# Expert outputs scattered tile by tile, and a regrouped step between two quantised attention passes

## The chip, the cores and the metric

The kernel runs on one core of a Trainium2 chip. The metric is device time in microseconds (us) from the start to the end of one execution. Three runs of the kernel before gave 2891.12, 2894.81 and 2895.28 us; their median is 2894.81 us. The profile comes from one further execution, which took 2868.81 us, with a span of 2867.1 us between its first and last record.

## The reference, cut to what matters

The model is a small tower: token embedding with a trace memory, linear attention, a soft mixture of experts, an attention block whose operands are fake-quantised to 8 bits, and last a transformer block with attention and a mixture of 8 experts of which each token uses two. There are B = 8 sequences of S = 512 tokens with D = 192 features. Two parts matter here.

```python
# quantised attention: per-tensor scale from the largest absolute value
def fake_quant(x, bits=8):
    scale = jnp.maximum(jnp.max(jnp.abs(x)) / 127.0, 1e-08)
    return jnp.clip(jnp.round(x / scale), -128, 127) * scale
attn = jnp.einsum('bhnd,bhmd->bhnm', fake_quant(q), fake_quant(k)) * scale
attn = fake_quant(jax.nn.softmax(attn, axis=-1))
out = jnp.einsum('bhnm,bhmd->bhnd', attn, fake_quant(v))

# routed experts: each token's two best experts, weighted by a softmax of their logits
top_logits, top_idx = jax.lax.top_k(xn @ gate_w, 2)
gates = scatter(softmax(top_logits))
y = gelu(xn @ w1[e] + b1[e]) @ w2[e] + b2[e]
out = x + sum over the two experts of gates * y
```

The softmax of the quantised attention has one scale for the whole tensor, so its maximum over all rows must be known before a single probability can be rounded. That is why this attention makes two passes over the scores.

## The kernel before, in words

The program is a list of stages, each made of blocks. In a block every engine has its own instruction list; the lists are written out by hand and run in order, engines meet only through semaphores, and all engines meet at the end of a block. Loops written with `Fori` are loops of the chip, others are unrolled. DMAs that `sp` issues go through SyncE's queue, those that `pool` issues through GpSimd's. `Link` (line 89) makes an instruction signal and the next one wait for it.

**Linear attention** (line 442) also fills the DRAM tensor `routed_in` with zeros (line 483), long before it is used, since the expert tiles are padded.

**Quantised attention** (line 1321). Pass 1 (lines 1641 to 1673) computes scores with queries on the partitions, takes each row's maximum (`MXq`) and, on ScalarE, the sum of exponentials (`RS`). Then a block of its own prepares pass 2 (lines 1684 to 1739): VectorE takes 1/RS and its maximum over all rows, GpSimd reduces it over partitions, and from it and ScalarE's logarithm follows one number for each query row, by which pass 2 shifts its scores so that the exponential gives the probability already in units of the quantisation step. The shift is split into three bf16 parts (`BP`, lines 1698 and 1703), turned by 32 TensorE transposes (1728), copied out of PSUM to `BT` (1707) and laid by DMA into three spare rows under each head's query features in `QI` (1738). Twelve heads sit in three groups `g` of four slots `q` of 32 partitions. Pass 2 (lines 1752 to 1844) computes the scores turned, with K spread by DMA into `QM` (1762) and V copied to `VS` (1764); the same five DMAs are made for each of the 8 sequences, two buffers alternating.

**Routed experts** (line 2368). After a layer norm (`XA` holds the rows) and the gate logits, one block works out for each of the 4096 tokens and its 2 experts a place `POS` in a list sorted by expert, in 39 tiles of 256 rows. GpSimd then sends the rows with 64 indirect DMAs of 128 rows (line 2532) to `routed_in`. The tile block (2609 to 2726) runs 39 tiles: SyncE loads a tile's rows (2621, 2622) and its expert's weights (2505, a ring of `NW` = 4), TensorE turns them (2652), multiplies by W1 (2662, 2666), ScalarE applies gelu (2701), TensorE multiplies by W2 (2677), VectorE adds the bias (2718), and GpSimd stores the tile to `routed_out` in sorted order (2637) and waits for the store before it frees the buffer `YM`. A last block gathers: 64 indirect DMAs (2739) fetch each token's two output rows by `POS`, VectorE adds both, weighted, to the residual (2751, 2755), and SyncE stores the result (2767).

## Time and profile before

| | |
|---|---|
| median of 3 runs | 2894.81 us |
| the profiled execution / its span | 2868.81 / 2867.1 us |
| busy: TensorE, VectorE, ScalarE, GpSimd | 69%, 53%, 39%, 11% of the span |
| between pass 1 and pass 2 of the quantised attention | 1334.6 to 1385.8 us |
| sending the rows to the experts | 2343 to 2426 us |
| the 39 tiles | 2426 to 2775 us |
| the last block | 2775 to 2867 us |

Shares of busy time are averages over stages with different limits. A change in one stage is judged by that stage's own rows: what ran, and what was waited for. The chain that ended last, as the profile follows it, covers only the last block here, so the other stages are read from the timeline.

### The profile page before, as it was taken

To read this page: it belongs to the slowest core of one execution; us is meant where nothing else is said; L and a number is where in the kernel's file an instruction comes from. 1 tells how busy PE (TensorE), PEld (TensorE's weight loads), DVE (VectorE), ACT (ScalarE), POOL (GpSimd) and SP (SyncE) were. 2 spreads that over 40 slices of the span, in tenths; PEclk is the share of its full clock that TensorE was granted. 3 is DMA by queue.
4 is the path that set the end of the run, shared out by engine and by line. 5 is a ranking of instruction groups with operands and counts; after the bars stand their busy time and mean duration, and the time that the engine had idled before them with its cause. 6 is when DMAs were issued, how large, how long until landed. Compare 5 with 4: busy or idle time off the path is not lost. (4 is left out here: it accounts for less than half of the span.)

```text
span 2867.1 us, 32319 instructions
## 1 busy us (share of the span) xinstructions
PE 1967.8 (69%) x9516; PEld 1035.9 (36%) x9538; DVE 1521.2 (53%) x2573; ACT 1124.2 (39%) x1862; POOL 312.9 (11%) x338
## 2 busy tenths in 40 slices
PE   4787788678873436664577648885799740999960
PEld 3645645353341100000111223321233340888850
DVE  4366378640026668886477738896477640111113
ACT  1102222231113579996588622220688410322210
POOL 4000000001110000000000042220000026000026
PEclk9899989777865655555799767775899755999985
DMA  3041100138930000000100048772898022455533
GB/s 71 11 137 39 42 17 22 54 146 311 411 151 11 0 15 11 11 11 2 36 26 29 1 77 114 105 105 30 117 111 109 3 95 79 174 200 209 202 105 107
DMA packets 140738, 251.39 MB, mean 88 GB/s; under 512 B 28762, under 2 KB 108251, under 8 KB 135628
## 3 DMA queue, kind: packets, MB, share of 16 engines
q1 hardware_dynamic: 128340, 225.99, 30.8%
q0 software_dynamic: 12304, 24.20, 2.9%
q8 instruction: 52, 0.85, 0.1%
q14 instruction: 42, 0.34, 0.0%
HBM read 194.69 MB, written 38.04 MB: 81 GB/s over the span
## 5 line engine op out<-in xcount | busy, mean ns | idle before, releaser
L1641 PE MATMUL ps<-arena 128*128 x376 | 194.3, 620 | 158.6 <-ACT ps L1673 96.0
L1673 ACT ACTIVATE ps<-ps,arena 128x512 f32<-128x512 f32 x384 | 291.8, 993 | 9.7 <-DVE arena L1652 9.7
L1658 DVE TENSOR_REDUCE arena<-ps 128x1024 f32 x192 | 234.4, 1224 | 47.9 <-PE ps L1641 46.5
L2032 DVE TENSOR_REDUCE arena<-ps 128x1024 f32 (+1 forms) x192 | 226.8, 1221 | 47.2 <-PE ps L2148 42.8
L1819 ACT ACTIVATE arena<-ps,arena 128x1024 f32<-128x1024 f32 x192 | 197.8, 1111 | 36.6 <-DVE arena L1841 27.3
L2313 ACT ACTIVATE arena<-ps 128x1024 f32<-128x1024 f32 x192 | 185.2, 1022 | 38.2 <-PE ps L2250 36.4
L2148 PE MATMUL ps<-arena 96*128 96x512 bf16 x384 | 159.7, 509 | 36.6 <-DVE arena L2032 23.6
L531 PE MATMUL ps<-arena 96*128 96x456 f32 (+1 forms) x512 | 176.5, 498 | 9.3 <-DMA arena<-arena 5.7
L2701 ACT ACTIVATE arena<-ps,arena 128x256 f32<-128x256 f32 x234 | 89.5, 481 | 235.9 <-PE ps L2666 235.9
L1841 DVE TENSOR_SCALAR arena<-arena 128x1024 bf16<-128x1024 f32 x192 | 130.8, 691 | 95.6 <-ACT arena L1819 79.0
L2718 DVE TENSOR_TENSOR arena<-ps,arena 128x384 f32<-128x384 f32 x39 | 21.7, 557 | 289.4 <-PE ps L2677 289.4
L1673 ACT ACTIVATION_READ_ACCUMULATOR ps<-ps,arena 128x1 f32 x384 | 171.6, 447 | 0.0
L2677 PE MATMUL ps<-arena 128*128 128x192 f32 x936 | 162.5, 331 | 0.7 <-DVE arena L2718 0.7
L2677 PEld LDWEIGHTS ps<-arena 128*128 128x128 f32 x936 | 151.0, 190 | 13.6 <-issue 13.6
L1781 PE MATMUL ps<-arena 128*128 (+1 forms) x370 | 117.3, 398 | 39.1 <-DMA arena<-arena 36.4
L1641 PEld LDWEIGHTS ps<-arena 128*128 128x128 bf16 x384 | 26.0, 112 | 326.3 <-ACT ps L1673 228.3
L2250 PE MATMUL ps<-arena 99*128 99x512 bf16 x384 | 103.2, 389 | 38.4 <-DMA arena<-arena 34.0
L531 PEld LDWEIGHTS ps<-arena 96*128 96x128 f32 x512 | 100.5, 205 | 76.6 <-issue 58.8
L2662 PE MATMUL ps<-arena 128*128 128x256 f32 x468 | 109.4, 384 | 0.9 <-ACT arena L2701 0.9
L1799 PE MATMUL ps<-arena 128*32 128x512 bf16 x384 | 77.5, 400 | 46.8 <-DVE arena L1841 38.6
L2288 PE MATMUL ps<-arena 128*32 128x512 f32 x768 | 103.5, 611 | 3.3 <-ACT arena L2313 3.3
L1204 DVE COPY arena<-ps 128x768 f32<-128x768 f32 x16 | 15.3, 957 | 159.9 <-PE ps L1246 159.9
(370 smaller groups left out, 3265.4 us busy)
## 6 DMA issues: line engine op xcount, KB each, us to landing
arena<-in_sm_w_dram SPq DMA_DIRECT2D x128, 576.0 KB
arena<-in_re_w_dram SPq DMA_DIRECT2D x39, 1252.0 KB, 5.7
arena<-ra_parts SPq DMA_DIRECT2D x192, 192.0 KB, 9.8
ra_parts<-arena SPq DMA_DIRECT2D x48, 192.0 KB, 2.5
routed_in<-arena SPq DMA_DIRECT2D x1, 7488.0 KB, 26.4
arena<-routed_in SPq DMA_DIRECT2D x39, 192.0 KB, 5.5
routed_out<-arena POOLq DMA_DIRECT2D x39, 192.0 KB, 2.3
arena<-la_xt SPq DMA_DIRECT2D x16, 384.0 KB, 3.3
```

The source lines that it names most:

```text
L531: ins = pe.matmul(ps[:, 2 * (t % 2) + bank, to:to + w], XTs[j][:, c, t * P:(t + 1) * P], Wx[:, kind, c, at:at + w], start=(c == 0), stop=( ...
L1641: ins = pe.matmul(ps[:, 2 * (n % 4) + t % 2, :], QM[j][:, h, t * P:(t + 1) * P], KI[:, b, h // HG, :], start=True, stop=True)
L1658: v.tensor_reduce(MXq[:, b, h, 2 * u:2 * u + 2], ps[:, 2 * (n % 4):2 * (n % 4) + 2, :], AX.X, ALU.max).then_inc(s_lk, 1)
L1673: ins = act.activation(bank, bank, ACT.Exp, bias=nb[n % 4][:, t % 2:t % 2 + 1], scale=c_exp, accum_out=RS[:, b, h, t:t + 1])
L1781: ins = pe.matmul(ps[:, 2 * (n % 3) + q, :], QM[j][:, h, c * P:(c + 1) * P], QI[:, bass.ds(b, 1), g, :].rearrange("p o s -> p (o s)"), sta ...
L1819: act.activation(PF[n % 2], ps[:, 2 * (n % 3):2 * (n % 3) + 2, :].rearrange("p a s -> p (a s)"), ACT.Exp, scale=c_exp).then_inc(pe_.sem, 1)
L1841: v.tensor_scalar(PB[n % 2], PF[n % 2], MAGIC, MAGIC, ALU.add, ALU.subtract).then_inc(rd.sem, 1)
L2032: v.tensor_reduce(MX[:, bass.ds(b, 1), 2 * (n % 2):2 * (n % 2) + 2, n // 2].rearrange("p o t -> p (o t)"), ps[:, 2 * (n % 2):2 * (n % 2) + ...
L2148: ins = pe.matmul(ps[:, t, :], ST_[j][0][0:KR, h, t * P:(t + 1) * P], ST_[j][1][0:KR, h, :], start=True, stop=True)
L2313: act.activation(PF[e // 2 % 2][:, 2 * (e % 2):2 * (e % 2) + 2, :], ps[:, 2 * (e % 3):2 * (e % 3) + 2, :], ACT.Exp, scale=HD ** -0.5).then ...
L2662: pe.matmul(unit(k), wr[:, k * P:(k + 1) * P], XT[j][:, 0, :], start=True, stop=False)
L2677: ins = pe.matmul(ps[:, 7, h * D:(h + 1) * D], HT[j][:, k, h * P:(h + 1) * P], wr[:, at:at + D], start=(k == 0), stop=(k == KH - 1))
```

## The change

**Shift rows.** The minimum of `RS` is taken and then one reciprocal of a 128 x 1 column, instead of 384 reciprocals per partition and a maximum. `RS` and `MXq` are laid out so that heads are innermost; the three casts and two subtractions each become one instruction over 128 x 384. The transposes now leave the three parts of one head in neighbouring rows of `BT`; the copy out of PSUM is halved between VectorE and ScalarE; and the 36 DMAs of one row become 12 DMAs of three rows. The K and V copies for the first two sequences of pass 2 are issued at the start of this block, and pass 2's loop starts at its third sequence.

**Routing.** Rows of `routed_in` grow from 192 to `RW` = 196 words; the first word is the number of the row of `routed_out` to which this row returns. GpSimd writes that word into `XA` with an iota for each of the two experts, so the 64 indirect DMAs are now ordered by expert choice `k`, and the second iota waits until the first 32 DMAs have landed. Padding rows carry numbers of spare rows, written in the earlier fill. In the tile block VectorE copies the two numbers per partition to `back` (four buffers), and GpSimd issues two indirect DMAs per tile (128 rows each) that scatter the tile's rows to token order, in place of one plain store. The row load waits for the copy of the turned rows (`xc`) instead of the transposes (`xt`), since `back` is read from the same buffer. In the last block 16 plain loads replace the 64 gathers, its loops are unrolled, and ScalarE's queue stores the result.

```diff
-            l(v.reciprocal(W_, RS))
-            v.tensor_reduce(pmax, W_, AX.XYZ, ALU.max).then_inc(s_b, 1)
+            l(v.tensor_reduce(pmax, RS, AX.XYZ, ALU.min))
+            v.reciprocal(pmax, pmax).then_inc(s_b, 1)
...
             for k in range(3):
-                for b in range(B):
-                    ins = v.tensor_copy(BP[:, b, :, k, :], turned(W_, b))
-                    if b == B - 1:
-                        l(ins)
+                l(v.tensor_copy(BP[:, :, :, k], W_))
                 if k < 2:
-                    for b in range(B):
-                        ins = v.tensor_tensor(turned(W_, b), turned(W_, b), BP[:, b, :, k, :], ALU.subtract)
-                    l(ins)
+                    l(v.tensor_tensor(W_, W_, BP[:, :, :, k], ALU.subtract))
...
-            v.tensor_copy(BT.rearrange("p (u b) s -> p u (b s)", u=4),
-                          ps[0:3 * NH, 0:4, :].bitcast(BF16)).then_inc(s_bc, 1)
+            v.tensor_copy(BT[:, 0:4, :].rearrange("p (u b) s -> p u (b s)", u=2),
+                          ps[0:3 * NH, 0:2, :].bitcast(BF16)).then_inc(s_bc, 1)
...
+            act.wait_ge(s_bt, 2)
+            act.activation(BT[:, 4:8, :].rearrange("p (u b) s -> p u (b s)", u=2),
+                           ps[0:3 * NH, 2:4, :].bitcast(BF16), ACT.Copy).then_inc(s_bc, 1)
...
-            for k in range(3):
-                for h in range(NH):
-                    row = 32 * (h % HG) + HD + k
-                    sp.dma_start(QI[row:row + 1, :, h // HG, :], BT[k * NH + h:k * NH + h + 1, :, :]
-                                 ).then_inc(s_q, 16)
+            for j in range(2):
+                spread(sp, j, j)
+            sp.wait_ge(s_bc, 2)
+            for q in range(HG):
+                for g in range(NG):
+                    row, at = 32 * q + HD, 3 * (q * NG + g)
+                    sp.dma_start(QI[row:row + 3, :, g, :], BT[at:at + 3, :, :]).then_inc(s_q, 16)
...
             for k in range(2):
-                pool.wait_ge(s_sc[k], 16 * NR)
+                if k:
+                    pool.wait_ge(s_sc[0], 16 * NR)
+                pool.iota(to_row, [[S, B], [1, T]], base=k * NT * P, channel_multiplier=T).then_inc(s_tr, 1)
+                pool.wait_ge(s_tr, k + 1)
+                if not k:
+                    pool.wait_ge(s_pl, 1)
+                for n in range(NR):
+                    pool.indirect_dma_start(xd, bass.IndirectOffsetOnAxis(ap=POS[:, n, k:k + 1], axis=0),
+                                            XA[:, n // T, n % T, :], None).then_inc(s_sc[k], 16)
...
             def load_rows(n):
-                xt.wait(sp, n, -1)
+                xc.wait(sp, n, -1)
...
-                pool.dma_start(yd_t[n], YM[j]).then_inc(m.ym[j], 16)
-                pool.wait_ge(m.ym[j], 16 * (n // 2 + 1))
+                for h in range(2):
+                    pool.indirect_dma_start(yd, bass.IndirectOffsetOnAxis(ap=back[n % 4][:, h:h + 1], axis=0),
+                                            YM[j][:, h, :], None).then_inc(m.ym[j], 16)
+                pool.wait_ge(m.ym[j], 32 * (n // 2 + 1))
...
             def rows(n):
                 xt.wait(v, n, 1)
+                if n >= 4:
+                    yf.wait(v, n, -3)
+                v.tensor_copy(back[n % 4], XM[n % 2].bitcast(I32)[:, :, 0])
                 hp.wait(v, n, -3)
...
-                v.wait_ge(s_y, b + 1)
+                v.wait_ge(s_g[b], 32)
...
+            for b in range(B):
+                for k in range(2):
+                    at = (k * B + b) * S
+                    sp.dma_start(Y[:, b, k, :, :], rows_of(yd[at:at + S])).then_inc(s_g[b], 16)
```

On SyncE's queue, in the block between the two passes, stood before (a row is a line, what it issues, its shape, and how often in a run; the last rows are the head of pass 2's loop):

```order
L1732 UNCONDITIONAL_BRANCH
L1738 DMA arena<-arena 1x8x512 x36
L1684 UNCONDITIONAL_BRANCH
L1754 UNCONDITIONAL_BRANCH
L1757 UNCONDITIONAL_BRANCH
L1757 ISA
L1762 ISA
```

The same place now, where 1758 is the line of the shift rows, 1699 of the K copies and 1701 of the V copies:

```order
L1750 UNCONDITIONAL_BRANCH
L1699 DMA arena<-arena 32x3x512 x4
L1701 DMA arena<-arena 128x1536
L1699 DMA arena<-arena 32x3x512 x4
L1701 DMA arena<-arena 128x1536
L1758 DMA arena<-arena 3x8x512 x12
L1703 UNCONDITIONAL_BRANCH
L1770 UNCONDITIONAL_BRANCH
L1772 UNCONDITIONAL_BRANCH
L1772 ISA
```

Ten copies moved ahead of the shift rows, and 36 DMAs of 1 x 8 x 512 became 12 of 3 x 8 x 512.

GpSimd's list from the sending of the rows (2532) over the tile stores (2637) to the last block's gathers (2739), before:

```order
L2524 AFFINE_SELECT arena<-arena 128x128
L2532 DMA routed_in<-arena 9984x192 x64
L2507 UNCONDITIONAL_BRANCH
L2631 UNCONDITIONAL_BRANCH
L2637 DMA routed_out<-arena 128x384 x39
L2616 UNCONDITIONAL_BRANCH
L2734 UNCONDITIONAL_BRANCH
L2739 DMA arena<-routed_out,arena 128x192 x64
```

The same stretch now, with the iotas on line 2543, the sending on 2548 and the scatter of the tiles on 2653:

```order
L2537 AFFINE_SELECT arena<-arena 128x128
L2543 IOTA arena 128x32
L2548 DMA routed_in<-arena 9984x196 x32
L2543 IOTA arena 128x32
L2548 DMA routed_in<-arena 9984x196 x32
L2520 UNCONDITIONAL_BRANCH
L2646 UNCONDITIONAL_BRANCH
L2653 DMA routed_out<-arena 8448x192 x78
L2631 UNCONDITIONAL_BRANCH
```

The 64 gathers of the last block are gone from this list; 39 more DMAs stand in the tile block, and an iota stands in the middle of the sending.

## Rows read from the trace of the kernel before

**Rows 1.** Windows: length, busy PE, PEld, DVE, ACT, POOL, clock, DMA share, GB/s
```profile
2339.00:2356.00 17.00, 0.00 (x0) 0.00 (x0) 2.81 (x8) 0.00 (x0) 10.00 (x11) 0.50 0.91 353
2500.00:2700.00 200.00, 200.00 (x1207) 176.16 (x1205) 27.54 (x48) 52.79 (x138) 12.94 (x24) 1.00 0.58 201
2774.70:2867.10 92.40, 0.00 (x0) 0.00 (x0) 29.51 (x72) 0.00 (x0) 63.76 (x64) 0.50 0.33 102
```

**Rows 2.** Timeline between the passes: start, duration, engine, line, idle before and its releaser
```profile
1334.94 2.55 DVE L1688 RECIPROCAL arena<-arena 128x384 f32<-128x384 f32 x1 [3.71 <-PEq L1616]
...
1338.57 0.15 DVE L1691 TENSOR_SCALAR arena<-arena 128x1 f32<-128x1 f32 x1 [0.49 <-POOL arena L1713]
...
1339.48 0.62 DVE L1694 SCALAR_TENSOR_TENSOR arena<-arena 128x384 f32<-128x384 f32 x1 [0.56 <-ACT arena L1718]
1340.14 0.97 DVE L1698 CAST arena<-arena 128x48 bf16<-128x48 f32 x8
...
1345.85 3.57 PE L1728 MATMUL ps<-arena 128*36 128x128 bf16 x32 [16.26 <-DVEq L1705]
1349.46 2.28 DVE L1707 COPY arena<-ps 36x4096 bf16<-36x4096 bf16 x1 [3.76 <-PE ps L1728]
1351.77 26.02 SPq L1738 DMA_DIRECT2D arena<-arena  x36
1378.90 1.28 ACT L1819 ACT_TABLE_LOAD   x1 [39.53 <-DVEq L134]
1379.40 3.08 SPq L1762 DMA_DIRECT2D arena<-arena  x4
...
1385.80 2.34 PE L1781 MATMUL ps<-arena 128*128 128x512 bf16 x5 [36.38 <-DMA arena<-arena]
...
1386.47 3.14 ACT L1819 ACTIVATE arena<-ps,arena 128x1024 f32<-128x1024 f32 x3 [6.28 <-PE ps L1781]
```

**Rows 3.** Line 1604, the one earlier DMA on three partitions: issue durations
```profile
L1604 SPq DMA_DIRECT2D arena<-arena x4: 786/1582/3449, 1023.2 to 1027.3; - x4
```

**Rows 4.** The same DMAs, by window while they move (columns as in rows 1)
```profile
1025.50:1035.50 10.00, 0.00 (x0) 0.00 (x0) 0.00 (x0) 1.28 (x1) 0.00 (x0) 0.50 0.20 34
```

**Rows 5.** Timeline of the last block and the store before it
```profile
2772.42 0.54 POOL L2637 DMA_DIRECT2D routed_out<-arena  x1 [4.34 <-DVE arena L2718]
2775.22 0.96 DVE L2751 TENSOR_TENSOR arena<-arena  x1 [3.10 <-PEq L2616]
...
2790.09 0.95 POOL L2739 DMA_INDIRECT arena<-routed_out,arena  x1 [0.30 <-issue]
...
2791.35 1.22 POOL L2739 DMA_INDIRECT arena<-routed_out,arena  x1 [0.30 <-issue]
...
2862.07 1.40 DVE L2755 SCALAR_TENSOR_TENSOR arena<-arena  x4 [0.18 <-DVE arena L2755]
```

**Rows 6.** DMA issues by kind: queue, count, KB each, median us from issue to landing
```profile
arena<-la_xt SPq DMA_DIRECT2D x16, 384.0 KB, 3.3
routed_out<-arena POOLq DMA_DIRECT2D x39, 192.0 KB, 2.3
arena<-routed_out,arena POOLq DMA_INDIRECT x64, 2.6
```

**Rows 7.** Line 2532: issue durations in ns, first and last start, landing
```profile
L2532 POOL DMA_INDIRECT routed_in<-arena x64: 956/960/1199, 2343.0 to 2422.9; - x64
...
DMA to landing us min/median/max: 2.3/2.3/7.4
```

**Rows 8.** Timeline, one tile of the loop, VectorE, GpSimd and SyncE
```profile
2560.19 0.56 DVE L2718 TENSOR_TENSOR arena<-ps,arena 128x384 f32<-128x384 f32 x1 [7.47 <-PE ps L2677]
...
2561.04 0.54 POOL L2637 DMA_DIRECT2D routed_out<-arena  x1 [8.08 <-DVE arena L2718]
2561.49 0.36 SPq L2505 DMA_DIRECT2D arena<-in_re_w_dram  x1
...
2569.66 0.54 POOL L2637 DMA_DIRECT2D routed_out<-arena  x1 [8.09 <-DVE arena L2718]
```

More of the change, by code:

```diff
@@ L1673, in _, with spread @@
                         ins = act.activation(bank, bank, ACT.Exp, bias=nb[n % 4][:, t % 2:t % 2 + 1],
-                                             scale=c_exp, accum_out=RS[:, b, h, t:t + 1])
+                                             scale=c_exp, accum_out=RS[:, b, t, at_head(h):at_head(h) + 1])
                     ins.then_inc(ex.sem, 1)
     g4 = Cut(m.arena, mark, END)
-    BP = g4(P, [B, T, 3, NH], BF16)
+    BP = TMP[:, S:S + 3 * B * T * NH // 2].bitcast(BF16).rearrange("p (n h k) -> p n h k", h=NH, k=3)
     BT = g4(3 * NH, [B, S], BF16)
-    W_ = TMP[:, 0:B * NH * T].rearrange("p (b h t) -> p b h t", b=B, h=NH)
+    W_ = TMP[:, 0:B * NH * T].rearrange("p (n h) -> p n h", h=NH)
+    rows = lambda a: a.rearrange("p b t h -> p (b t) h")
     s_a, s_b, s_c, s_ln, s_bp, s_bt, s_bc, s_q = (sem(f"qa_shift_{n}") for n in (
         "chain", "max", "max_of_all", "log", "parts", "turned", "copied", "rows"))
+    km = [sem(f"qa_k_spread{j}") for j in range(2)]
+    def spread(sp, b, j):
+        for q in range(HG):
+            sp.dma_start(QM[j][32 * q:32 * q + 32].rearrange("p (g j) s -> p g j s", j=HG)[:, :, q, :],
+                         KI[32 * q:32 * q + 32, b, :, :]).then_inc(km[j], 16)
+        sp.dma_start(VS[j], VI[:, b, :, :, :]).then_inc(km[j], 16)
     with nc.Block(no_gpsimd_drain=True) as block:
@@ L1755, in _ @@
         def _(sp):
-            sp.wait_ge(s_q, 16 * 3 * NH)
-            with sp.Fori(0, B // 2) as i:
+            with sp.Fori(1, B // 2) as i:
                 for j in range(2):
-                    b = 2 * i + j
                     prev(sp, av, i, j)
-                    for q in range(HG):
-                        sp.dma_start(QM[j][32 * q:32 * q + 32].rearrange("p (g j) s -> p g j s", j=HG)[:, :, q, :],
-                                     KI[32 * q:32 * q + 32, b, :, :]).then_inc(km[j], 16)
-                    sp.dma_start(VS[j], VI[:, b, :, :, :]).then_inc(km[j], 16)
+                    spread(sp, 2 * i + j, j)
         @block.tensor
@@ L2420, in norm @@
                 ins.then_inc(xa.sem, 1)
[L2422 removed]
+                rows = XA[:, bass.ds(b, 1), :, HEAD:RW].rearrange("p o t d -> p (o t) d")
                 xa.wait(v, b, 1)
@@ L2606, in routed_experts @@
     two = lambda shape: [w(P, shape) for _ in range(2)]
-    XM, XT, HT, YM = two([2, 2 * P]), two([2, TR]), two([KH, TR]), two([2, D])
+    XM, XT, HT, YM = two([2, HEAD + 2 * P]), two([2, TR]), two([KH, TR]), two([2, D])
+    back = [w(P, [2], I32) for _ in range(4)]
     xm = [sem(f"re_rows_loaded{j}") for j in range(2)]
@@ L2764, in _ @@
         def _(sp):
-            with sp.Fori(0, B) as b:
-                sp.wait_ge(s_f, b + 1)
-                sp.dma_start(io.out[bass.ds(b, 1)].rearrange("o (p t) d -> (o p) (t d)", t=T),
-                             m.H[:, b, :, :].rearrange("p t d -> p (t d)")).then_inc(s_o, 16)
-            sp.wait_ge(s_o, 16 * B)
+            for b in range(B):
+                for k in range(2):
+                    at = (k * B + b) * S
+                    sp.dma_start(Y[:, b, k, :, :], rows_of(yd[at:at + S])).then_inc(s_g[b], 16)
+        @block.scalar
+        def _(act):
+            for b in range(B):
+                act.wait_ge(s_f, b + 1)
+                act.dma_start(rows_of(io.out[b]), m.H[:, b, :, :]).then_inc(s_o, 16)
+            act.wait_ge(s_o, 16 * B)
 def kernel_program(nc, io):
```

91 lines of the change are left out of this document (40 added, 51 removed).

## The prediction

> **What bounds the kernel now.** I read the windows first [rows 1]. While the tiles run, TensorE is busy in all 200 of 200 us at full granted clock (2.4 GHz), GpSimd in 12.9: what the change adds to GpSimd there has room, and nothing there can be won. In the last block TensorE is idle, VectorE is busy 29.5 of 92.4 us and GpSimd 63.8: the gathers set its pace. Then the timeline between the two passes [rows 2]: from the reciprocal at 1334.94 to the first exponential of pass 2 at 1386.47 there is one chain and nothing beside it. Its longest link is SyncE's 36 DMAs, 26.02 us at 0.72 each. Every microsecond cut from these two chains comes off the end, since all engines meet at the end of a block.
>
> **The step between the passes, VectorE's part.** The reciprocal falls from 384 elements to one: from 2.55 us to about the 0.15 of a 128 x 1 operation, -2.4. The minimum costs what the maximum did. The split took from 1340.14 to 1345.85, 5.7 us. Now it is three casts and two subtractions of 128 x 384, each at most the 0.62 of the SCALAR_TENSOR_TENSOR of that size, together 3.1, -2.6. The transposes (3.57 us) stay. Of the copy (2.28 us for 4096 columns) VectorE's half hides beside the second 16 transposes; ScalarE's half of 2048 columns comes behind them. One ScalarE instruction of 1024 columns takes 1.05 us (3.14 for three), so at most 2.1, and no less than half of VectorE's 2.28, 1.14. I take 2.1, by the ScalarE row: -0.2. The shift rows can then start at 1351.77 - 5.2 = 1346.6 [rows 2].
>
> The ten K and V copies now ahead of them on SyncE's queue are issued from 1335 on: four take 3.08 us [rows 2], all ten about 7.5, so they are through at 1342.5, under VectorE's chain.
>
> **The shift rows.** By the issue alone, 12 times 0.72 make 8.7 us. Each DMA now carries three rows of 8 KB. The only earlier DMA on three partitions is line 1604: four of 72 KB, whose issues took 0.79, up to 3.45 us [rows 3], so SyncE was held up by the transfer. While they moved, the DMA share was 0.20, about three engines of 16, and the rate 34 GB/s [rows 4]. The 288 KB of the shift rows at 34 GB/s take 8.7 us as well, as long as the issues. The upper end is line 1604's own pace: 0.79, 3.45 and two around the median of 1.58 make 7.4 for four, 1.85 each, 22.2 for twelve, though those carry three times the bytes. Below 8.7 I see no way, because SyncE must issue twelve. I take 10.2, near the lower end, since by bytes the two limits agree and only their overlap is imperfect.
>
> The Trainium skill (DMA: Bandwidth & Descriptors, section "Why a DMA increments its semaphore by 16 and not by 1") says that the engines of a DMA are the largest number up to 16 that divides both slowest dimensions. By that rule a 3 x 8 x 512 transfer uses three engines where a 1 x 8 x 512 used eight; it speaks against the regrouping, and the share of 0.20 agrees with it. It would make the transfer, not the issue, the limit, which is the first rival.
>
> The issues end at 1356.8. Now the next DMA that waits for the rows starts 1.6 us after the last issue ended (1377.79 to 1379.40), so the rows have landed at 1358.4; the first matmul about 0.4 later (my allowance for waking TensorE and its weight load), and the exponential 0.67 behind it as now (1385.80, 1386.47) make 1359.5. ScalarE's table load began 1.1 us after the last issue and takes 1.28 [rows 2]: done at 1359.2, just covered. The K and V copies that stood here (1379.40 to 1385) are already in place. Pass 2 starts at 1359.5 and not 1386.47: **-27.0**. The ends are -29.5 (ScalarE's copy at 1.14, transfer at 8.7) and -15.0 (22.2 for the DMAs). The changed layouts of `MXq` and `RS` move writes of two elements or one; pass 1 and pass 2 keep their pace.
>
> **The last block.** Now it begins 2.8 us after the last store is issued (2772.42, 2775.22). A second DMA 1.26 us behind the first (0.95 + 0.30 [rows 5]) and a landing of 2.6 instead of 2.3 us [rows 6] put the begin at 2776.8. The second of the two loads for the first sequence is issued 0.6 later and lands 3.3 us on, as the 384 KB load from DRAM does [rows 6]: 2780.7, first weighted sum at 2780.8. A sequence then costs VectorE 0.96 + 1.40 + 0.18 + 1.40 = 3.94 us [rows 5]. The first sum pair takes 3.0, seven more sequences 27.6: 2811.4. From VectorE's last instruction (2863.5) to the end now is 3.6 us. End at 2815.0 against 2867.1: **-52.1**.
>
> What could hold this back is the transfer: 6.3 MB in and 3.1 MB out. At 353 GB/s, as the four weight loads moved [rows 1], that is 26.7 us, less than VectorE's 3.0 + 27.6, but not by much. At the 201 GB/s of the tile loop, which there is demand and not a limit [rows 1], it would be 47 us, and the block 13 longer than forecast: -39. The other end is -54, if the first loads land in 1.3 us less.
>
> **Sending the rows.** The 64 issues keep 1.27 us (2343.0 to 2422.9, 63 steps [rows 7]); 784 instead of 768 bytes a row don't matter to an issue-bound stretch. New is the stop between `k` = 0 and 1: instead of one step of 1.27 the last landing of 2.3 [rows 7], the iota with its signals, 0.4, and a first issue of 1.2 against 0.96. **+1.7**, between +1 and +3. The first iota stands ahead of the wait for `POS`.
>
> **The tiles.** Per tile VectorE gets one more copy of 128 x 2, about 0.15 us, and idles 7.5 [rows 8]; it counts only ahead of the first tile, where both turns wait for it: **+0.4**, ends 0 and 1. The row load waits about 0.7 us longer for its tile, but it is issued well over a tile ahead, behind a wait for `yc` that ends later. GpSimd: one store at 0.54 us becomes two scatters, 0.95 + 0.30 + 0.95. It starts at 2561.04, and the next tile is due at 2569.66 [rows 8]. The second scatter is issued at 2562.3; with 2.3 to 2.6 us of landing [rows 6, 7] GpSimd is free at 2565, 4.6 us early. But the weights start at 2561.49. With weights under way, a scatter of line 2532 landed in up to 7.4 us [rows 7]; there four experts' weights were queued, here one's. Then it would be free at 2569.8, 0.2 to 0.5 us late. I take nothing. New on VectorE is that the copy to `back` waits for the store of the tile before the last; queued behind it are the copy of the turned rows, for which TensorE waits only a tile later, and the next bias addition.
>
> The Trainium skill (SBUF — State Buffer, section "SBUF: two separate sides") says that GpSimd can't write descriptors while VectorE runs a two-port copy. This trace shows up to 0.27 us of it (1.22 instead of 0.95 while VectorE works [rows 5]); in the tile loop it would lie in GpSimd's 4.6 spare us, and the sum would be the same.
>
> **The sum.** -27.0 - 52.1 + 1.7 + 0.4 = -77.0. The profiled execution of 2868.8 us becomes 2791.8. The runs' median lies 26.0 above it; I keep that distance: 2894.8 - 77.0 = 2817.8, so 2818.
>
> **The rivals.**
> 1. Three-partition transfers set the pace: line 1604's held-up issues speak for it, the equal 8.7 us by bytes against. At the middle of the two ends, 16 us instead of 10.2: 2824; at the full 22.2, 2830.
> 2. The last block is bound by its transfers: all 16 loads are queued at once and the stores share the engines; against it stand 353 GB/s and long contiguous runs. At 201 GB/s, 2831.
> 3. The scatter paces the tiles mildly: a landing of 7.4 us makes the cycle 0.5 us longer than TensorE's 8.62, times 39 is +20: 2838. Against it: one expert's weights are a quarter of what stood before that 7.4.
> 4. Slower than before: the same place in earnest. GpSimd waits for both scatters before it frees `YM`, VectorE waits for that, TensorE for VectorE. The 77 us are lost when the cycle reaches 8.62 + 77/39 = 10.6 us, that is a landing of about 9. If scattered rows of 768 bytes among the weights landed in 10 us, it would be 11.7 and +120: 2938. No row shows such a landing.
> 5. It doesn't do what it says: the loads can't start early or the shift rows cost as before. Then only one of the two large terms comes, 2845 to 2870.
>
> **Chances.** Forecast 0.64, rivals 0.11, 0.10, 0.08, 0.04, 0.03. The best ends together give 29.5 + 54 - 1 = 82.5, 2812; the distance of 26 us to the runs is uncertain by their spread of 4, so I start the range at 2808. Upward it takes in rivals 1 to 3: 2838. What a measurement can tell from no change is 0.2%, 6 us. Only rival 4, below its full price too, can come out there or beyond: faster 0.94, same 0.02, slower 0.04.
>
> **What would show it.** In the profile after: first exponential of pass 2 about 25 us after the minimum; the twelve issues in 9 to 11 us (right) or 16 and more (rival 1); eight sequences at 3.9 us each in the last block, VectorE not waiting for loads; a single gap of about 3 us in the sending; tiles still 8.62 us apart with TensorE busy throughout. Tiles further apart than 8.8, or a last block over 45 us, would make the prediction wrong.

## The result, and the profile after

The kernel after takes 2802.77 us (median of 4 runs, 2798.69 to 2814.05) against 2894.06 us before, a ratio of 0.9692 with a 95% interval of 0.9663 to 0.9721: 91 us less, where the forecast was 77. It lies 5 us under the low end of the forecast range. The direction and the main mechanism were forecast, the time was not.

The windows of the kernel after, in the columns of [rows 1]: the twelve shift-row DMAs, the tile loop and the last block.

```profile
1356.00:1366.00 10.00, 0.00 (x0) 0.00 (x0) 0.00 (x0) 0.00 (x0) 0.00 (x0) 0.54 0.13 27
...
2500.00:2700.00 200.00, 200.00 (x1208) 176.28 (x1207) 28.36 (x69) 54.07 (x142) 44.09 (x46) 1.00 0.60 204
2763.10:2800.60 37.50, 0.00 (x0) 0.00 (x0) 29.54 (x72) 0.00 (x0) 0.00 (x0) 0.50 0.67 252
```

The tile loop is what it was, TensorE busy throughout, with GpSimd at 44 instead of 13 us of 200. The last block is 37.5 us long, VectorE busy in 29.5 of them (before in 29.5 of 92.4), and the transfers run at 252 GB/s.

The step between the passes, timeline of the kernel after (it answers to [rows 2]):

```profile
1344.82 2.66 SPq L1699 DMA_DIRECT2D arena<-arena  x4
...
1344.86 0.55 DVE L1707 TENSOR_REDUCE arena<-arena 128x1 f32<-128x384 f32 x1 [3.71 <-PEq L1625]
1345.44 0.16 DVE L1708 RECIPROCAL arena<-arena 128x1 f32<-128x1 f32 x1
...
1350.53 3.26 PE L1745 MATMUL ps<-arena 128*36 128x128 bf16 x32 [11.02 <-DVEq L1719]
...
1353.83 1.87 ACT L1734 ACTIVATE arena<-ps 36x2048 bf16<-36x2048 bf16 x1 [6.92 <-PE ps L1745]
1355.72 9.77 SPq L1758 DMA_DIRECT2D arena<-arena  x12
1366.42 1.28 ACT L1830 ACT_TABLE_LOAD   x1 [10.73 <-DVEq L136]
1368.53 0.13 PEld L1792 LDWEIGHTS ps<-arena 128*128 128x128 bf16 x2 [14.92 <-DMA arena<-arena]
...
1369.61 2.12 ACT L1830 ACTIVATE arena<-ps,arena 128x1024 f32<-128x1024 f32 x2 [1.90 <-PE ps L1792]
```

From the minimum to the first exponential: 24.75 us (forecast 24.6; before 51.5). The twelve issues take 9.77.

The last block, timeline of the kernel after (it answers to [rows 5]):

```profile
2759.21 0.96 POOL L2653 DMA_INDIRECT routed_out<-arena  x1 [2.66 <-DVE arena L2738]
2760.47 0.96 POOL L2653 DMA_INDIRECT routed_out<-arena  x1 [0.30 <-issue]
2763.11 8.96 SPq L2776 DMA_DIRECT2D arena<-routed_out  x16
2763.15 0.96 DVE L2759 TENSOR_TENSOR arena<-arena 128x768 f32<-128x768 f32 x1 [4.22 <-PEq L2631]
2767.16 2.85 DVE L2763 SCALAR_TENSOR_TENSOR arena<-arena 128x192 f32<-128x192 f32 x8 [3.05 <-DMA arena<-routed_out]
...
2771.50 2.85 DVE L2763 SCALAR_TENSOR_TENSOR arena<-arena 128x192 f32<-128x192 f32 x8 [0.62 <-DMA arena<-routed_out]
...
2775.25 2.85 DVE L2763 SCALAR_TENSOR_TENSOR arena<-arena 128x192 f32<-128x192 f32 x8
```

The first weighted sum comes 4.0 us after the begin, as forecast; a sequence then takes 3.75 us (2771.50 to 2775.25; forecast 3.94, because the 0.18 us between two groups of four is gone). Behind the first load, which the forecast waited for too, only the second sequence waits, 0.62 us.

Sending and one tile, GpSimd, VectorE and SyncE of the kernel after (they answer to [rows 7] and [rows 8]):

```profile
2368.41 0.96 POOL L2548 DMA_INDIRECT routed_in<-arena  x1 [0.30 <-issue]
2370.80 0.18 POOL L2543 IOTA arena<- 128x32 int32 x1 [1.44 <-DMA routed_in<-arena]
2371.26 0.98 POOL L2548 DMA_INDIRECT routed_in<-arena  x1 [0.28 <-POOL arena L2543]
...
2564.24 0.56 DVE L2738 TENSOR_TENSOR arena<-ps,arena 128x384 f32<-128x384 f32 x1 [7.39 <-PE ps L2694]
2564.71 0.16 DVE L2730 COPY arena<-arena 128x2 int32<-128x2 int32 x1
...
2565.07 0.96 POOL L2653 DMA_INDIRECT routed_out<-arena  x1 [6.40 <-DVE arena L2738]
...
2566.33 0.96 POOL L2653 DMA_INDIRECT routed_out<-arena  x1 [0.30 <-issue]
...
2572.86 0.56 DVE L2738 TENSOR_TENSOR arena<-ps,arena 128x384 f32<-128x384 f32 x1 [7.40 <-PE ps L2694]
```

One gap of 2.85 us from issue to issue in the sending; the tiles are 8.62 us apart, as before.

Where the time lies, as differences between the first instructions of the stages. The middle column is the kernel before, unchanged, in another execution (run e1 below).

| us | before, trace shown | before, run e1 | after |
|---|---|---|---|
| embedding stage | 136.6 | 145.5 | 146.2 |
| to the end of pass 1 | 1198.4 | 1198.3 | 1198.6 |
| minimum to first exponential | 51.5 | 51.5 | 24.8 |
| pass 2 | 227.0 | 226.9 | 228.6 |
| to the routing's first iota | 709.9 | 710.3 | 710.9 |
| iota to last sending DMA | 99.6 | 99.6 | 101.4 |
| to the first bias addition | 25.2 | 25.1 | 24.4 |
| 39 tiles | 323.5 | 323.5 | 323.5 |
| last bias addition to the end | 95.5 | 110.7 | 42.2 |
| span | 2867.1 | 2891.4 | 2800.6 |

The first and third columns differ by the forecast's terms, -26.8 and -53.3 among them, and by +9.6 us in a stage that the change doesn't touch. The first two columns are the same kernel, and differ in two rows: 8.9 and 15.2 us.

### The profile page after: what moved, and what is told of

Read it like the earlier page. It is cut to its first block and busy times, and to the rows that moved or that the text cites. A ratio compares the mean times of both kernels' runs of the same rounds, so it can differ in the third digit from the quotient of the medians.

```text
span 2800.6 us, 32083 instructions
## 1 busy us (share of the span) xinstructions
PE 1964.5 (70%) x9516; PEld 1031.1 (37%) x9538; DVE 1518.9 (54%) x2578; ACT 1125.9 (40%) x1863; POOL 302.7 (11%) x316
## 5 line engine op out<-in xcount | busy, mean ns | idle before, releaser
L1650 PEld LDWEIGHTS ps<-arena 128*128 128x128 bf16 x384 | 25.6, 110 | 326.6 <-ACT ps L1682 228.6
L2653 POOL DMA_INDIRECT routed_out<-arena x78 | 74.8, 958 | 275.2 <-DVE arena L2738 256.2
## 6 DMA issues: line engine op xcount, KB each, us to landing
routed_in<-arena SPq DMA_DIRECT2D x1, 7644.0 KB, 24.6
```

The source lines that it names most:

```text
L1650: ins = pe.matmul(ps[:, 2 * (n % 4) + t % 2, :], QM[j][:, h, t * P:(t + 1) * P], KI[:, b, h // HG, :], start=True, stop=True)
```

## The experiments

### The parts, and the kernel before once more (e1 to e4, on one chip)

e1 is the kernel before, unchanged.

> The kernel before, unchanged, profiled once more. The question is why its timed runs (2891 to 2895 us) lie 25 us above its one profiled execution (2868.8), while the timed runs of the changed kernel lie around its profiled one. Theory A (the profiled execution was an unusually short one; upstream stages vary from one execution to the next): the new profiled execution comes out near 2893, and its trace shows the extra 20 to 25 us in stages that the change does not touch, the embedding stage first (136.6 us in the trace shown). Theory B (the profiler itself shortens or lengthens this program): the new profiled execution is again near 2869 while the timed ones stay near 2893.

Measured: 2893.16 us (10 runs), 2894.36 for the same kernel beside it, span 2891.4. The execution first shown was a short one; so far theory A, though the runs further below put it down to the chip and not to the execution. But its missing time lies in two places, the embedding stage and the last block, and the second belongs to what the change removes.

e2 has the new step between the passes alone; of the change's diff, for one:

```diff
-                    sp.dma_start(QI[row:row + 1, :, h // HG, :], BT[k * NH + h:k * NH + h + 1, :, :]
-                                 ).then_inc(s_q, 16)
...
+                    sp.dma_start(QI[row:row + 3, :, g, :], BT[at:at + 3, :, :]).then_inc(s_q, 16)
```

> Only the step between the two quantised passes is changed. By the traces the step gives 26.8 us and pass 2 takes 1.9 of them back, so theory A expects 24 to 28 us less than before, about 2867 where before is at 2893. A rival by which the timed gain of 91 us hides a larger effect of this step than its trace shows expects 35 us or more.

Measured: 2866.24 us, ratio 0.9895 (0.9878 to 0.9913), 28 us less, the upper edge of theory A's range. First exponential 24.91 us after the minimum for 51.5, pass 2 1.7 us longer.

e3 has the routing alone (rows that carry their address, the scatter in each tile, plain loads at the end), and the step between the passes as before:

```diff
+                    pool.indirect_dma_start(yd, bass.IndirectOffsetOnAxis(ap=back[n % 4][:, h:h + 1], axis=0),
+                                            YM[j][:, h, :], None).then_inc(m.ym[j], 16)
...
+                    sp.dma_start(Y[:, b, k, :, :], rows_of(yd[at:at + S])).then_inc(s_g[b], 16)
```

> Only the routing is changed (rows carry their return row, tiles are scattered, the last block loads plain rows). By the traces: last block and its begin -53.3, sending +1.6, tile loop about 0: 51 to 53 us less, about 2841 where before is at 2893. A rival by which the unexplained 14 us of the timed gain belong to the routing (for example to instruction fetch in the looped last block) expects 65 us less.

Measured: 2825.55 us, ratio 0.9761 (0.9745 to 0.9777), 69 us less. My expectation failed; the rival named in it, that the unexplained time belongs to the routing, is what happened.

e4 is the kernel after.

> The changed kernel, unchanged, profiled once more. Theory A (the embedding stage varies between executions) expects that its embedding stage does not take 146.2 us again to a tenth, and the total moves with it by some us; a rival (the changed program always has the longer embedding stage, through where its instructions lie) expects 146 us again, and 137 in the kernel before.

Measured: 2800.42 us, ratio 0.9679 (0.9663 to 0.9695), 94 us less; the parts make 28 + 69 = 97. Its embedding stage takes 143.7 us, not 146.2, as theory A expected, but the kernel before has 145.5 there in e1 and not 137. So the stage is long in both kernels, and its length varies.

What differs in the last block of before between its two executions stands in a view of one line's instructions (min/median/max in ns, first and last start). Line 2755 in the execution first shown, and behind it in e1:

```profile
L2755 DVEq FUSED_REGOPS  x96: 65/93/105, 2787.6 to 2862.4; - x96
L2755 DVE SCALAR_TENSOR_TENSOR arena<-arena x64: 408/412/420, 2787.9 to 2863.1; - x64
```

```profile
L2755 DVEq FUSED_REGOPS  x96: 1/93/1396, 2796.6 to 2886.7; - x96
L2755 DVE SCALAR_TENSOR_TENSOR arena<-arena x64: 408/415/477, 2796.9 to 2887.3; - x64
...
  issue: 48.7, 21
```

Line 2749, the loop's own, in e1:

```profile
L2749 DVEq ALU_OP  x8: 11/40/700, 2799.0 to 2886.9; - x8
L2749 DVEq COMPARE_BRANCH  x8: 40/56/700, 2799.0 to 2886.9; - x8
```

The timeline of e1 from the last gather on, GpSimd and VectorE:

```profile
2866.08 0.94 POOL L2739 DMA_INDIRECT arena<-routed_out,arena  x1 [0.30 <-issue]
...
2870.44 0.42 DVE L2755 SCALAR_TENSOR_TENSOR arena<-arena  x1 [2.39 <-issue]
2872.62 1.12 DVE L2755 SCALAR_TENSOR_TENSOR arena<-arena  x3 [1.76 <-issue]
...
2886.35 1.41 DVE L2755 SCALAR_TENSOR_TENSOR arena<-arena  x4 [0.18 <-DVE arena L2755]
```

The arithmetic is as fast as ever, and the gathers are too: the last one is issued 82 us into the block in both. But from 2810.9 to 2873.2, 46 of the 62 register and branch instructions of VectorE and SyncE take 0.70 us each (one 1.40) for 0.04 to 0.10. From 2819.9 on their starts lie on one grid of 0.70 us, for both engines alike: SyncE's at 2826.3, 2827.7 and 2829.1, VectorE's at 2826.3, 2828.4, 2829.8 and 2831.2. The same grid shows in e2 and e13. Without the slow ones, VectorE ends 4.9 us behind the last gather (2858.55 to 2863.47); with it, 20.7 us. From 2876 on, the gathers landed, a pair of groups is back at 3.0 us.

### Loop and gathers, one without the other (e5, e6, e13, e16)

e5 is the kernel before with the loops of VectorE and SyncE in the last block written out:

```diff
-            with v.Fori(0, B) as b:
-                link = Link(v, s_a, b * 2)
+            link = Link(v, s_a)
+            for b in range(B):
...
-                       scalar=GT[:, bass.ds(T * b + t, 1), k], in1=m.H[:, b, t, :],
+                       scalar=GT[:, T * b + t, k:k + 1], in1=m.H[:, b, t, :],
...
-            with sp.Fori(0, B) as b:
+            for b in range(B):
```

> The kernel before with one edit: in the last block VectorE's loop over the 16 sequences and SyncE's loop of stores are written out, so that neither engine has register or branch instructions there; the 128 gathers of GpSimd stay. In every new execution of the kernel before, these register instructions took 0.70 us each beside the gathers (46 of them, 33 us) and the block 107 us; in the execution that the forecast started from none did and the block took 92 us. Theory A (these instructions, slowed beside the gathers, are what the forecast missed): 15 us less, a median of 2878 us (2874 to 2882), the block again at 92 us, the embedding stage as before at 144 to 147 us. Rival B (everything on VectorE is slowed there and the register instructions are only where it is seen): other instructions take over the time, the block stays at 105 to 107 us and the median at 2889 to 2896 us.

Measured: 2879.35 us (2875.93 to 2882.62), 15.0 less than the 2894.33 beside it; block 92.1 us, embedding stage 146.6. Theory A in all three numbers. (The kernel has 64 gathers and 8 sequences here; the 128 and 16 above, and the 16 in e6, are slips.)

e6 is the kernel after with the loop back, and no gathers:

```diff
+            with v.Fori(0, B) as b:
+                link = Link(v, s_a, b * 2)
-                v.wait_ge(s_g[b], 32)
+                v.wait_ge(s_y, b + 1)
...
+        @block.gpsimd
+            for b in range(B):
+                pool.wait_ge(s_g[b], 32)
+                pool.sem_inc(s_y, 1)
```

> The kernel after with one edit: in the last block VectorE's code is a loop over the 16 sequences again, with register instructions, while GpSimd issues no gather there (it only passes a semaphore on). Theory A (register instructions are slow only beside GpSimd's indirect DMAs): each takes under 0.1 us, the block takes 38 to 41 us for 37.4, and the median is 1 to 3 us above the kernel after (2801 to 2806 us). Rival B (a loop is slow in this place whatever GpSimd does, 0.70 us for each of some 46 register instructions): 10 to 15 us more, a median of 2811 to 2816 us.

Measured: 2804.91 us (2804.47 to 2806.91), block 40.4 us for 37.4, as theory A expected, and its register instructions are short:

```profile
L2763 DVEq FUSED_REGOPS  x96: 65/93/99, 2766.4 to 2798.2; - x96
```

So it takes both: loop with gathers 107.0 us, gathers without loop 92.1, loop without gathers 40.4, neither 37.4. The loop costs 15 us beside the gathers and 3 without them.

e13 (the kernel before, unchanged) and e16 (e5's kernel) ran on a third chip, after a chip had shown the lower level (below).

> The kernel before, unchanged, for its trace on this chip. Theory A (the two levels belong to the chip): its time is that of all runs of the kernel before beside it, near 2869 or near 2893 us; at the lower level no register instruction of the last block takes over 0.1 us, that block takes 92 us and the embedding stage 134 to 138 us; at the upper level 46 take 0.70 us, the block takes 107 us, the stage 144 to 147 us. Rival B (the levels belong to single executions): both kinds show among the runs of one chip.

> The kernel before with the last block's VectorE and SyncE loops written out, once more. Theory A (the 15 us that this saved were register instructions, slowed beside the gathers on chips of the upper level alone): on a chip where the kernel before takes 2869 us it takes 2865 to 2870 us, nothing or at most a few us less; where that takes 2893 us, 2876 to 2882 us. Rival B (the loop costs its 15 us everywhere): 2854 us on the first kind.

Measured: e13 2893.87 us, block 107.0, stage 147.7; e16 2875.57 us (2874.97 to 2881.38), 19 less than the 2894.34 beside it, block 89.7. Theory A's upper level in both; the times between this chip's runs don't mix the levels. e16 lies 0.4 us below the range given.

### The embedding stage (e7)

The kernel after with VectorE's loop there written out:

```diff
-                with v.Fori(B // 4 * half, B // 4 * (half + 1)) as i:
+                for i in range(B // 4 * half, B // 4 * (half + 1)):
```

> The kernel after with one edit: VectorE's loop over pairs of sequences in the embedding stage is written out. Nine or ten of its register instructions take 0.70 to 0.84 us each beside GpSimd's gathers of embedding rows in every execution but the one that the forecast started from (6.3 to 8.4 us in all; the stage takes 144 to 147 us for 136.6 us there). Theory A: the stage is back at 136.5 to 139 us, and the median 6 to 9 us lower than that of the kernel after, 2791 to 2795 us. Rival B (the gathers set the stage's pace and VectorE's slow instructions lie in its waits): less than 2 us, 2799 to 2802 us.

Measured: 2798.38 us (2794.92 to 2802.18), 2 us under e4's 2800.42 and not told from it (the ratios, each to the kernel before on its own chip, are 0.9674 and 0.9679). Theory A failed. Rival B's range is missed by 0.6 us, which the spread of the runs doesn't settle. The slow register instructions are gone, and yet the stage takes 142.9 us (143.7 in e4, and 147.2 in e15, which has the same edit). Something else holds it. ScalarE's instruction for the second sequence, in the first trace of before, then in the kernel after:

```profile
44.15 0.49 ACT L324 ACTIVATE arena<-ps 128x384 f32<-128x384 f32 x1 [4.72 <-PE ps L358]
```

```profile
51.12 0.49 ACT L326 ACTIVATE arena<-ps 128x384 f32<-128x384 f32 x1 [11.92 <-remote]
```

In e7, ScalarE and VectorE both stand still and start within 0.04 us of each other:

```profile
42.81 0.81 PE L360 MATMUL ps<-arena 128*128 x2
...
50.79 1.25 DVE L278 TENSOR_SCALAR arena<-arena 128x192 f32<-128x192 f32 x4 [12.57 <-remote]
50.83 0.49 ACT L326 ACTIVATE arena<-ps 128x384 f32<-128x384 f32 x1 [11.96 <-remote]
```

Both wait for TensorE, whose products end at 43.6, and both go on at 50.8, about 3 us after the last gather of the embedding (47.08 + 0.95). This pause of 7 us is in all 15 traces from chips whose kernel before took 2893 to 2898 us, with ScalarE's start at 50.8 to 51.3, and in none of the other five. The trace's own record of the semaphore says where it arises: the increment that VectorE waits for belongs to a product that ends at 42.98, and is recorded at 50.76. It is 7.0 to 9.0 us behind its product in those 15 traces, 0.01 to 0.02 in the other five. So by these records the signal is late, and not the engines that wait for it.

The same traces lack records. The 32 gathers of this stage raise their semaphores 512 times (16 each); 231 to 254 of these are recorded in the 15 traces, 507 to 512 in the other five. So one rival is open: that on these chips the recording itself holds the engines up. Every run here, timed ones too, has a span that comes from such records, and no run without them stands against it.

### Two levels, by chip (e14, e17, e18)

On the chip of e9 to e12, the kernel before took 2869.29 us in the median of 15 runs (2861.66 to 2874.75). On the five other chips of these experiments it took 2887.0 to 2902.2 in all of 69 runs. None of the four traces from that chip has a register instruction over 0.5 us, nor the pause (ScalarE's instruction starts at 42.4 to 43.7), and their embedding stage takes 133.9 to 137.7 us. The trace that the forecast started from is of this kind (2868.81 us); the runs shown beside it were of the other. To get the kernel after on such a chip, it went to further chips:

> The kernel after, unchanged. Theory A: on a chip where the kernel before takes 2869 us, it takes 2791 to 2795 us (the sum of the forecast, 77 us less, a ratio of 0.973); on a chip where that takes 2893 us, 2799 to 2803 us (94 us less, a ratio of 0.9675). Rival B (the change is worth the same on both kinds of chip): 2775 us on the first kind.

> The kernel after, unchanged, on one more chip. Theory A (the level belongs to the chip): where the kernel before beside it takes 2869 us, 2791 to 2795 us, a ratio of 0.973; where that takes 2893 us, 2799 to 2803 us and 0.968. Rival B (the change is worth 94 us everywhere): 2775 us and 0.967 on the first kind.

> The kernel after, unchanged, on one more chip. Theory A (the level belongs to the chip): where the kernel before beside it takes 2869 us, 2791 to 2795 us, a ratio of 0.973; where that takes 2893 us, 2799 to 2803 us and 0.968. Rival B (the change is worth 94 us everywhere): 2775 us and 0.967 on the first kind.

Measured: all of the upper level, 2801.64, 2799.31 and 2803.07 us; ratios 0.9680 (0.9655 to 0.9705), 0.9671 (0.9655 to 0.9687) and 0.9672 (0.9656 to 0.9688). The ratio is the same on every chip of that kind. The kernel after itself was not run at the lower level, so what theory A and rival B say of it stayed untested. The nearest is e9, 2798.33 us there; its duplicates cost 4.6 us behind the last tile and nothing in the tiles, so after would take 2793.7, 75.6 less than before. From e11 (below), 2794.04 us with a step 4.9 us longer, it would be 2789.1, 80 less. Both are worked out, not measured.

### The prices in the forecast (e8 to e12, e15)

e8: the kernel after, its 12 three-row DMAs cut into 36 of one row.

```diff
-                    sp.dma_start(QI[row:row + 3, :, g, :], BT[at:at + 3, :, :]).then_inc(s_q, 16)
+                        sp.dma_start(QI[row:row + 1, :, g, :], BT[at:at + 1, :, :]).then_inc(s_q, 16)
```

> The kernel after with the 12 DMAs of three partition rows each between the quantised passes cut into 36 of one row each; the bytes are the same. Theory A (SyncE's issues set the pace of these copies, 0.76 us each with a floor of 0.61 us): 24 more issues, the first exponential of pass 2 comes 15 to 18 us later than the 24.8 us after the minimum, the median 2815 to 2819 us. Rival B (what is paid is the bytes through the SBUF side of three partitions, and the issues only queue behind it): the exponential 0 to 3 us later, the median 2800 to 2804 us.

The issues in e8's timeline:

```profile
1354.29 26.01 SPq L1759 DMA_DIRECT2D arena<-arena  x36
```

Measured: 2814.80 us (2810.41 to 2815.93); first exponential 39.3 us after the minimum for 24.8. Theory A's mechanism, with both numbers just under its ranges (14.5 us for 15 to 18): 0.60 us for each further issue.

e9 and e10: each tile's scatters twice and three times.

```diff
-                for h in range(2):
-                    pool.indirect_dma_start(yd, bass.IndirectOffsetOnAxis(ap=back[n % 4][:, h:h + 1], axis=0),
+                for h, y in [(h, y) for y in [yd] + io.spare for h in range(2)]:
+                    pool.indirect_dma_start(y, bass.IndirectOffsetOnAxis(ap=back[n % 4][:, h:h + 1], axis=0),
```

> The kernel after with twice the scatters: in each tile GpSimd issues four indirect DMAs for two, the second pair with the same rows and the same indices into a spare tensor that nobody reads. Theory A (the scatters run in slack: a tile's 8.62 us are set elsewhere, and n scatters close their cycle in about 0.26 + 1.264 n + 2.3 to 2.6 us): four close in 7.3 to 7.7 us, the tiles stay 8.62 us apart and the median within 2 us of the kernel after (2799 to 2804 us). Rival B (the scatters' bytes or descriptors slow the other transfers or VectorE): the tiles come more than 0.1 us further apart, over 4 us in all, 2805 us or more.

> The kernel after with three times the scatters (six indirect DMAs for two in each tile, four of them into two spare tensors that nobody reads). Theory A: six close their cycle in 9.8 to 10.2 us, GpSimd sets the pace of the 39 tiles, the 8.62 us become 9.8 to 10.2 and the median 2846 to 2862 us. Rival B (the buffers of two tiles let the landing overlap with the next tile's issue, so that only 6 x 1.264 = 7.6 us of issue count): no change, 2799 to 2804 us.

Measured: e9 tiles still 8.62 us apart; 2798.33 us; e10 10.29 us apart, 2876.07 us. GpSimd, e9 then e10:

```profile
2505.52 0.96 POOL L2653 DMA_INDIRECT routed_out<-arena  x1 [3.83 <-DVE arena L2738]
...
2509.32 0.96 POOL L2653 DMA_INDIRECT spare<-arena  x1 [0.31 <-issue]
2514.22 0.96 POOL L2653 DMA_INDIRECT routed_out<-arena  x1 [3.93 <-DMA spare<-arena]
```

```profile
2504.11 0.96 POOL L2653 DMA_INDIRECT routed_out<-arena  x1 [3.15 <-DMA spare<-arena]
...
2510.43 0.96 POOL L2653 DMA_INDIRECT spare<-arena  x1 [0.30 <-issue]
```

The mechanism of theory A holds, its size doesn't: from the last issue's end to the next tile's scatter it takes 2.8 to 3.9 us (2510.28 to 2514.22), not 2.3 to 2.6. Those two counted from an issue's start, and the expectation added them to its end; besides, from the start the scatters land after 4.8 us in the median of e9 and 3.7 in e10. So four scatters already close in 8.7 us, just at the tile's pace, and six cost 82 us (against the 2793.7 us worked out above) rather than some 55, above the range. I also left out what waits behind the last tile: 4.6 us in e9, 14.4 in e10.

e11: the kernel after with the K and V copies behind the shift rows.

```diff
-            for j in range(2):
-                spread(sp, j, j)
             sp.wait_ge(s_bc, 2)
...
+            for j in range(2):
+                spread(sp, j, j)
```

> The kernel after with SyncE's ten copies of K and V for pass 2 moved behind the 12 DMAs of the shift rows; nothing else changes. Theory A (issues queue on SyncE, 0.6 to 0.8 us each, and the copies were free where they stood because SyncE waited there anyway): five of the ten are needed by the first product, the first exponential comes 3 to 5 us later than the 24.8 us after the minimum, and the median is 2803 to 2807 us. Rival B (the copies compete with the shift rows for the transfers, and both orders cost the same): within 1 us, 2799 to 2802 us.

SyncE and ScalarE in e11:

```profile
1344.90 9.76 SPq L1756 DMA_DIRECT2D arena<-arena  x12
1354.70 2.76 SPq L1699 DMA_DIRECT2D arena<-arena  x4
...
1360.86 0.60 SPq L1701 DMA_DIRECT2D arena<-arena  x1
1362.31 1.28 ACT L1830 ACT_TABLE_LOAD   x1 [17.44 <-DVEq L136]
```

Measured: first exponential 29.7 us after the minimum, 4.9 later, within theory A's 3 to 5: the table load waits until SyncE has issued all ten. The median, 2794.04 us, is of the lower level and no higher than the 2793.7 worked out above: pass 2 (227.0 us) and the stages behind it (708.0) are 1.6 and 2.9 us shorter than after's. In pass 2 the trace shows why: TensorE's granted clock stands at the lower of its two levels (1.2 GHz) for 12.9 us there, and for 17.8 in after. The range was made for the upper level, and the total doesn't settle the price.

e12 and e15: six of the twelve DMAs issued by ScalarE, and e7's edit.

```diff
+    def shift_rows(eng, half):
+        eng.wait_ge(s_bc, 2)
+        for q in range(2 * half, 2 * half + 2):
...
+            shift_rows(act, 1)
...
+            shift_rows(sp, 0)
```

> The kernel after with two edits: VectorE's loop of the embedding stage written out (as tried before, 2 to 3 us), and six of the 12 DMAs of the shift rows issued by ScalarE, which is idle there, while SyncE issues the other six. Theory A (the issues, 0.76 us each, set the pace): the first exponential of pass 2 comes 4 to 5 us sooner, 20 to 21 us after the minimum, and the median is 2791 to 2795 us, below both kernels. Rival B (the bytes through three partitions set the pace, 24 KB in 0.8 us, whoever issues them): the exponential stays at 24 to 25 us, the median 2796 to 2800 us.

> The kernel with the shift rows issued by two engines and the embedding loop written out, once more. On a chip where the kernel before takes 2869 us: 2781 to 2785 us, as measured before; where that takes 2893 us: 6 to 9 us under the kernel after, 2792 to 2796 us. The rival, that the earlier 2782.75 us was the chip's level alone and the edits are worth under 3 us, gives within 3 us of the kernel after beside it.

Measured: 2782.75 us (2781.49 to 2783.45) beside before's 2869.29, ratio 0.9700 (0.9682 to 0.9718); on another chip 2796.36 us (2794.00 to 2801.51), ratio 0.9660 (0.9640 to 0.9679), where after took 2801.64. The step in e12:

```profile
1343.09 4.92 SPq L1708 DMA_DIRECT2D arena<-arena  x6
1343.10 5.81 ACTq L1708 DMA_DIRECT2D arena<-arena  x6
1349.88 1.28 ACT L1834 ACT_TABLE_LOAD   x1 [6.81 <-DVEq L136]
1352.02 0.13 PEld L1796 LDWEIGHTS ps<-arena 128*128 128x128 bf16 x2 [11.04 <-DMA arena<-arena]
```

First exponential 20.9 and 21.0 us after the minimum for 24.8 and 25.0: theory A. The totals fit less well. 2782.75 us is 8 us under the range given, which was made for the upper level; 2796.36 is 0.4 above its own, and 5.3 under after's for 6 to 9, which is more than the rival's 3. This is the fastest of the versions; the 4 us of the step are shown by the traces, the 5 us of the total not by intervals, which overlap.

## Why the prediction was wrong

**The step that failed** is the last of the sum: "The runs' median lies 26.0 above it; I keep that distance". It took 26 us between a profiled execution and the timed runs for a constant. It is no constant: 9 us of it is the embedding stage, which both kernels keep, and 15 us is VectorE's loop beside the gathers, and the change removes both. That the last block's loops are written out was known, and the forecast gave it no term. Against the trace that it was made from, the sum itself was near, as the terms show.

- **Between the passes**: forecast -27.0, measured -26.8. Its parts were off and cancelled: the shift rows start 10.9 us after the minimum (forecast 11.7), the issues take 9.8 (10.2), and from their end to the exponential 4.1 (2.7; the landing is 3.0, not 1.6).
- **The last block with its begin**: forecast -52.1. From the last tile's store to the end it went from 94.7 to 41.4 us, -53.3, by the first trace; by e1's it is -68.5 (110.7 to 42.2 from the last bias addition on). The 15 us between are the whole miss.
- **Sending** +1.8 (forecast +1.7). **Tiles** 0.0, and -0.8 between the last sending DMA and the first bias addition (forecast +0.4).
- **Not forecast**: pass 2 is 1.5 to 1.8 us longer in every kernel with the new step but e11 (0.0) and e12 (0.8). It goes with the granted clock: at the lower level for 14.9 to 15.0 us of pass 2 in all traces with the old step (226.9 to 227.0 us), 16.9 to 18.1 in those of 228.5 to 228.7 us, 12.9 in e11 and 14.9 in e12. Why the same step leaves other clock stretches is open. The +1.0 in the stages behind it is no more than their scatter, 707.4 to 711.0 us among the traces with the new step.

The forecast terms measured make -26.8 - 53.3 + 1.8 - 0.8 = -79.1 for -77.0; with +1.6 and +1.0, +9.6 in the embedding stage and +0.3 up to the end of pass 1 that is -66.6, the difference of the two spans (2867.1 and 2800.6) but for rounding. Against e1, where the last row is -68.5 and the embedding stage +0.7, it is the 91 us that the runs show.

**The rivals.** Rival 1, transfers of three partitions set the pace: no. Two engines issue the same 12 DMAs in 5.8 us for 9.8, at 41 GB/s for 27, and the landing stays at 3.1 us. The Trainium skill (DMA: Bandwidth & Descriptors, section "Why a DMA increments its semaphore by 16 and not by 1") gives three DMA engines for such a shape. The DMA share of 0.13, two engines of 16 on average, doesn't contradict it; the rows moved fast enough all the same. Rival 2, the last block bound by its transfers: no, 0.62 us of waiting behind the first load, at 252 GB/s. Rivals 3 and 4, the scatter paces the tiles: not with two. But the margin was smaller than the 4.6 us in the forecast: with the 2.8 to 3.9 us that four and six scatters took it is 2.5 to 3.6. Rival 5: no. One row beside them was misread: 1.22 us is not the longest gather of the last block, the first took 1.47, and beside both VectorE ran an addition and no copy. In the tile loop of after all 78 scatters are issued in 0.95 to 0.96 us, also where VectorE's copy runs at their start (2564.78 for 0.68 us, 2565.07), so no row shows GpSimd held up by VectorE there.

**The range.** Its low end took the best of my terms and 4 us of spread. It had no case in which the profiled execution was of another kind than the runs, though the 26 us said so plainly: six times the spread of the runs.

## What to carry to other kernels

When the profiled execution and the timed runs differ by much more than the runs among themselves, find out where before adding a difference to either; here one row of register instructions at 0.70 us would have shown it, in a trace of the right kind. Loops with register arithmetic are cheap (3 us for this block) until they stand beside many indirect DMAs of GpSimd (15 to 19 us, on the two chips where that was tried); write them out there, or take the gathers away. Whether that holds without recording isn't shown. Many small DMAs between two dependent steps cost their issues: join them, and give half to an idle engine's queue.

## What the runs showed of the hardware

- Beside GpSimd's indirect DMAs, from 26 to 33 us after they begin (a single one of SyncE's at 16 or 17), most register and branch instructions of VectorE and SyncE take 0.70 us instead of 0.04 to 0.10, on one grid of 0.70 us, in the last block of before on both chips of the upper level that traced it, and VectorE's in the embedding stage on all five; on the sixth chip never. Arithmetic keeps its time. The Trainium skill (Runtime: NRT & Kernel Launch, section "Instruction fetch mechanics") says that a taken branch to a page that isn't loaded stalls the engine. By that the loop's branches would be long, or what stands behind them; of the 46 in e1, 41 are register arithmetic. And the DMA queue that the profile names "instruction" (q14) moved one packet in the last block in e1 as in the first trace. So it doesn't explain this.
- On the same five chips VectorE and ScalarE went on 7 us late after TensorE's products in the embedding stage, 2.6 to 4.4 us behind the last gather's issue, and TensorE's increments are recorded 7.0 to 9.0 us late; that the gathers are the cause isn't shown. Half of the gathers' own increments are missing from these traces.
- From issue to issue SyncE takes 0.72 us with one partition (e8) and 0.81 with three (after); with ScalarE issuing beside it SyncE keeps 0.82, and ScalarE takes 0.97 on average (its first issue alone 1.65; e12).
